# Setup of a decoder block: rotated biases ahead of two weights' low parts, and the value bias' output projection ahead of the int8 weights' transposes

## What is computed

```python
x = x + attn(layernorm(x), Wq, bq, Wk, bk, Wv, bv, Wo, bo)      # 16 heads, causal, RoPE on q and k
x = x + xattn(layernorm(x), ctx, wq, bq, wkv, bkv, wp, bp)      # q and output in fake int8 (qdq)
x = x + moe(layernorm(x), router_w, w_gate, w_up, w_down)       # 64 experts, top 8, capacity 128
# in attn:  q = rope(h @ Wq.T + bq);  k = rope(h @ Wk.T + bk);  v = h @ Wv.T + bv
#           y = softmax(q k / sqrt(d), causal) v;   return y @ Wo.T + bo
# in xattn: qdq(w) = clip(round(w / s), -127, 127) * s,  s = max(|row|) / 127
```

## Time and profile before

| | |
|---|---|
| median of 3 runs | 1580.34 us (1577.61 to 1582.30) |
| profiled execution | 1569.49 us, span from its first to its last instruction 1567.4 us |
| mean granted TensorE clock | 0.960 |
| PE busy | 1405.6 us (90%) |
| DVE busy | 1166.1 us (74%) |
| ACT busy | 970.7 us (62%) |
| POOL busy | 673.5 us (43%) |
| chain that ended last | PE 66%, DMA 23%, issue 5%, DVE 3% |

### The profile page before, as it was taken

The page is one execution under the profiler, slowest core; times in us unless marked ns, Lnnn a source line. Parts: engine busy times, 40 slices in busy tenths (PEclk is TensorE's granted clock), DMA queues, the critical chain, the costliest instruction groups (busy, mean ns, idle before and its releaser), DMA issues.

```text
span 1567.4 us, 35601 instructions
## 1 busy us (share of the span) xinstructions
PE 1405.6 (90%) x10963; PEld 1062.5 (68%) x10996; DVE 1166.1 (74%) x3111; ACT 970.7 (62%) x3345; POOL 673.5 (43%) x654
## 2 busy tenths in 40 slices
PE   3499999999999999999999999999719888888895
PEld 2367777777777777777777777777516555655573
DVE  5768888999899998999989999988624444444453
ACT  3357777777777777777777777777604333333342
POOL 0011454444544434535345453444443554555556
PEclk9799999999999999999999999999859999999998
DMA  9681233222211110111111011100597999999964
GB/s 294 255 312 42 97 136 119 99 105 88 90 40 38 41 34 27 27 34 35 39 27 27 27 34 41 33 21 22 187 328 220 284 266 279 283 273 281 265 100 50
DMA packets 159737, 195.80 MB, mean 125 GB/s; under 512 B 39541, under 2 KB 121845, under 8 KB 159680
## 3 DMA queue, kind: packets, MB, share of 16 engines
q1 hardware_dynamic: 120768, 157.27, 30.6%
q0 software_dynamic: 38912, 37.87, 11.9%
HBM read 127.60 MB, written 130.29 MB: 165 GB/s over the span
## 4 chain that ended last, share of the span: by engine, by line
PE 66%; DMA 23%; issue 5%; DVE 3%; ACT 1%; POOL 1%; SPq 1%; POOLq 0%; DVEq 0%
PE bank L502 34%; DMA out<-x,slots 20%; PE bank L527 7%; PE bank L484 7%; PE bank L520 5%; PE bank L534 4%; PE bank L508 3%; PE bank L540 2%; PE bank L515 2%; DMA x_in<-in_x 1%; PE bank L489 1%; DMA wide_b<-in_xkT_w 1%; POOL routed L1753 1%; ACT probs L966 1%; DMA probsT<-in_oT_w 1%
## 5 line engine op out<-in xcount | busy, mean ns | idle before, releaser
L966 ACT ACTIVATE probs<-bank,small 128x128 f32<-128x128 f32 x1024 | 362.1, 377 | 48.3 <-DVE small L1270 45.0
L1753 POOL DMA_INDIRECT routed<-row,slots x248 | 253.8, 1023 | 133.5 <-issue 73.7
L1822 POOL DMA_INDIRECT out<-x,slots x128 | 198.9, 1554 | 194.8 <-DMA out<-x,slots 140.5
L1718 POOL TENSOR_TENSOR small<-small,half 128x1 f32<-128x1 f32 x96 | 54.6, 569 | 523.6 <-DVE small L1242 523.6
L966 ACT ACTIVATION_READ_ACCUMULATOR probs<-bank,small 128x1 f32 x1024 | 220.7, 216 | 0.0
L960 ACT ACTIVATE probsT<-bank 128x512 f32<-128x512 f32 x256 | 143.9, 610 | 88.5 <-PE bank L527 88.5
L1270 DVE TENSOR_REDUCE small<-bank 128x4 f32<-128x512 f32 x256 | 166.7, 682 | 33.8 <-PE bank L520 33.8
L527 PE MATMUL bank<-idf,probs 128*128 128x128 f32 x1024 | 146.8, 277 | 2.7 <-ACT probs L966 2.4
L1673 DVE TENSOR_SCALAR slots<-pairs 128x1 uint32<-128x1 f32 x128 | 13.7, 149 | 172.0 <-DMA out<-x,slots 168.4
L527 PEld LDWEIGHTS bank<-idf,probs 128*128 128x128 f32 x1024 | 121.7, 144 | 27.0 <-DVE probs L1279 3.8
L1200 ACT ACTIVATE xn<-bank 128x192 f32<-128x192 f32 x64 | 21.3, 332 | 147.4 <-PE bank L906 147.4
(11 more groups left out here) (242 smaller groups left out, 3838.4 us busy)
## 6 DMA issues: line engine op xcount, KB each, us to landing
w_gate_up<-in_w_gate SPq DMA_DIRECT2D x128, 192.0 KB, 3.6
w_gate_up<-in_w_up SPq DMA_DIRECT2D x128, 192.0 KB, 3.9
w_down<-in_w_down SPq DMA_DIRECT2D x128, 192.0 KB, 4.3
routed<-empty_row SPq DMA_DIRECT2D x4, 5120.0 KB, 22.0
x_in<-in_x SPq DMA_DIRECT2D x32, 256.0 KB, 2.6
ctx_sb<-in_ctxT_in SPq DMA_DIRECT2D x32, 256.0 KB, 3.0
x_res<-in_x SPq DMA_DIRECT2D x32, 256.0 KB, 2.5
out<-x SPq DMA_DIRECT2D x32, 256.0 KB, 2.0
```

Of the source, the lines that this page charges most:

```text
L966: last = act.activation(probs[:, g, j * P:(j + 1) * P], bank[:, b, j * P:(j + 1) * P], ACT.Exp, bias=negated[:, h:h + 1], **({"accum_out": ...
L1753: pool.indirect_dma_start(routed, bass.IndirectOffsetOnAxis(ap=slots_of(m)[:, k:k + 1], axis=0), row_of(m)[:, :], None, bounds_check=SLOTS ...
L1822: pool.indirect_dma_start(out.rearrange("b p (h c) -> (b p h) c", h=2), bass.IndirectOffsetOnAxis(ap=place_of[k % 2][:, half_:half_ + 1], ...
```

## The change

On SP the two bias broadcasts move from behind weight 1 to behind the loads of `body(2)`, ahead of weights 4 to 7. On DVE the low parts of weights 4 and 5 move from ahead of the rotation of the biases to behind it. On PE the twelve matmuls of the value bias move to the head of `turn_quantised_weights`, into bank 7 instead of bank 0, behind a wait for the low parts and the spread value bias. DVE makes `att_bias` ahead of the scales' diagonal instead of behind everything, and PE's matmuls of line 868, which write the same bank 7, wait for it. ACT's counts shift by one; PE's wait for ACT's three copies now stands ahead of `body(3)`.

```diff
@@ sync
             stage_weights(0)
             stage_weights(1)
-            load_biases()
             stage_weights(2)
             stage_weights(3)
             load_constants()
             body(2)
+            load_biases()
             for n in range(len(STAGE), len(matrices_in)):
                 stage_weights(n)
@@ tensor
             def turn_quantised_weights():
+                pe.wait_ge(s_lo_dve, len(weights_in))
+                pe.wait_ge(s_vspread, 1)
+                project(7, attT_hi, attT_lo, "o", 0, True, False)
+                project(7, attT_hi, attT_lo, "o", 1, False, False)
+                project(7, attT_hi, attT_lo, "o", 2, False, True).then_inc(s_wT, 1)
                 for n, staged in enumerate((roped[:, :], packed[:, :])):
...
                 pe.wait_ge(s_wprep, 3)
+                pe.wait_ge(s_att, 1)
                 for g in range(KT):
...
                 last.then_inc(s_wT, 1)
-                pe.wait_ge(s_lo_dve, len(weights_in))
-                pe.wait_ge(s_wTr, 3)
-                pe.wait_ge(s_vspread, 1)
-                project(0, attT_hi, attT_lo, "o", 0, True, False)
-                project(0, attT_hi, attT_lo, "o", 1, False, False)
-                project(0, attT_hi, attT_lo, "o", 2, False, True).then_inc(s_wT, 1)
...
             pe.wait_ge(s_const, 16 * N_CONST)
-            pe.wait_ge(s_att, 1)
+            pe.wait_ge(s_wTr, 3)
             for cur in range(3, 7):
@@ scalar
-                act.wait_ge(s_wT, n + 1)
+                act.wait_ge(s_wT, n + 2)
...
-            act.wait_ge(s_wT, 3)
+            act.wait_ge(s_wT, 4)
             act.activation(xp_row[:, :], bank[:, 7, :], ACT.Copy).then_inc(s_wTr, 1)
...
-            act.wait_ge(s_wT, 4)
             for cur in range(3, 7):
@@ vector
             body(2)
-            weights_lo(4)
-            weights_lo(5)
             dve.wait_ge(s_ident, 16)
             dve.wait_ge(s_const, 16 * N_CONST)
             dve.wait_ge(s_bias, 32)
...
+            weights_lo(4)
+            weights_lo(5)
             spread_v = v_bias[:, :].unsqueeze(2).to_broadcast([P, KT, P])
...
+            dve.wait_ge(s_wT, 1)
+            dve.tensor_tensor(att_bias[:, :], bank[:, 7, :], xatt[:, :], ALU.add).then_inc(s_att, 1)
             for g in range(KT):
                 last = dve.tensor_scalar(xn2[:, g * P:(g + 1) * P], idf[:, :], xp_ws[:, g:g + 1], None, ALU.mult)
...
             dve.wait_ge(s_wT, 4)
-            dve.tensor_tensor(att_bias[:, :], bank[:, 0, :], xatt[:, :], ALU.add).then_inc(s_att, 1)
             for cur in range(3, 7):
```

## The result

The changed kernel took 1569.80 us (median of 11 runs, 1564.86 to 1574.18) where the kernel before, run beside it, took 1577.61 (11 runs, 1576.11 to 1582.30). The ratio is 0.9943, with an interval of 0.9931 to 0.9956: 9 us by the ratio, 7.8 by the medians. Most of those 2.3 us are the base: the forecast started from a median of three runs, 1580.34, and over 11 runs the kernel before has 1577.61. From that base the same difference gives 1569.4.

A forecast was written before the change was run, and what follows sets the result against it. Setup and pipeline filling ahead of DVE's `body(3)` were taken to bound the gain: 3.7 us from DVE's order plus 4.5 from PE's made 8.2, so 1580.34 became 1572.1 us; own range 1569.7 to 1574.5, full range 1567.5 to 1577.8.

The forecast's parts named there:

- What bounds, and where: Setup ahead of 62 us: idle holes on DVE and PE; the question was how much earlier DVE's `body(3)` starts.
- Part 1: SP's order: second x tile at 25.2 us, bias broadcasts priced at 1.6 us, o weight 0.57 us later.
- Rival 1: Broadcasts behind the x tile cost 3.7 to 5.2 us, giving 1574.2 to 1575.7 us; chance 0.18.
- Part 2: DVE's order: the 4.24 us bias rotation fills the hole, first row maximum 3.7 us earlier, at 38.5.
- The dear form: Broadcasts at 5.2 us, o weight landing at 36.9: DVE's reordering then gains only 0.1 us.
- Part 3: Value bias' twelve matmuls on PE move earlier, hidden behind DVE: 4.5 us off ahead of `body(3)`.
- The carry: Behind DVE's `body(3)`, the whole 8.2 us lead passes down the pipeline; clearing queue empty with 3.9 us margin.
- Its distance from the median: The runs' median stays 10.85 us above the profiled execution: 1561.3 profiled, 1572.1 median.
- rival 2: TensorE's clock still full at xp's transposes: 1.3 us more gain, 1570.8 us; chance 0.06.
- Rival 3: Fourth x tile lands at 96.3 whatever DVE does, queue still clearing: 1580.3 us, no change; chance 0.11.
- Rival 4: xq weight completes only with the clearing quarter issued behind it: 8.5 us slower, 1588.8; chance 0.05.
- Rival 5: Broadcasts land after DVE's hole, so DVE's reordering does nothing; no chance of its own.

The follow-up runs named there:

- the second pair of profiles: Kernel before and changed kernel profiled again on the third chip, nothing else changed: one run of 1578.62 us against a median of 1567.67, ratio 0.9944.
- PE's part alone: Kernel before with only the value bias' matmuls and `att_bias` moved, SP and DVE as before; ratios 0.9972 and 0.9973 to the kernel before.
- all but SP's: Changed kernel with one line, `load_biases()`, moved back to its early place; ratios 0.9960 and 0.9944 to the kernel before.

## Why the prediction was right

- **What bounds, and where.** Right: the lead is made ahead of 62 us. The hole on PE closed as described. DVE's two waits went from 3.42 us to 2.57, in three pieces; the gain came from taking the rotation off the path behind o, which is what the term counted.
- **Part 1.** The direction of each step was right, two sizes were not. The second x tile came at 24.44, not 25.2: its lead is 1.8 us, where only SP's issue time of 1.06 was counted. The tile's load is issued behind DVE's first x normalisation, which stands behind the low part of xk and had moved by 1.63 us (22.87 to 21.24); the working named that move and did not use it. The pair's price in the new place was set at 1.6 us, by its row among megabyte weights; in the same terms, from tile to o, it was 2.83, so o is 2.83 - 1.80 = 1.03 late, and over five executions the price was 2.3 to 4.4. The failing step is "in the new place, as in the old, megabyte weights stand in the queue beside the pair": ahead of the pair stand the twelve constants and the tile, and the windows of 101 to 166 GB/s were the nearer row. Rival 1, with 0.18, came near in two of five executions (prices of 4.1 and 4.4 in its range of 3.7 to 5.2); its own sign, o at 35 or later, was met in one (35.56, the other 34.89). The Trainium skill (DMA: Bandwidth & Descriptors, Queues, rings and completion order) was taken to make the cheap price the likelier; no trace here shows it in the new place, and none shows on which rings the time went.
- **Part 2.** 3.7 said, 3.21 measured (o 1.03 late instead of 0.57), 1.5 in the second pair of profiles (42.32 to 40.78). Of the signs, "no idle before xv's low part" failed (1.39 us) and "under 1 us before o's" held (0.35). The dear form was priced at 0.1 from o at 36.9; it came to 35.6 at most, since the tile came earlier than counted and the pair cost 4.4, not 5.2.
- **Part 3.** 4.5 said, 4.53 measured between the two profiled executions: 7.74 less 3.21. Over all executions the term was too small (4.5 to 6.7), because the old place ran at the half clock three times in four. The row of 3.15 us was one execution's, and nothing in the working bounded it from above. Wrong too was "over 2 us to spare, even at the half clock": 2.0 to 2.5 us is what PE waits for DVE's rounding where the matmuls run at full clock (2.46 in after), and 0.9 to 1.2 where they run at half clock (0.93 in the second profile). It was enough. This and part 2's shortfall are of opposite sign, which is part of why the sum came out.
- **The carry.** "Whole" was wrong by 2.2 us in the profiled pair. The clearing's queue took 33.29 us instead of 31.85, and set the fourth tile; that is 1.44. The 0.9 us that PE had lost by then (its mask took 1.89 us, in before 1.15) was hidden in DVE's wait for the tile. Another 0.8 went right behind the tile, where the twenty matmuls shown above took 6.48 us instead of 5.71: PE starts at half clock in after (granted 0.50 from 94 to 98 us) and at full clock in before, where it fell only within 101 to 102. In the second pair nothing was lost: from second normalise to 6th load it is 87.13 us before and 87.00 after. This stretch varies from 85.0 to 88.6 us over all kernels with two quarters in `body(3)`, so the loss is of the size of that scatter; it may still be more than that, since the five executions with both DVE's and PE's part have 88.0 in the mean and the four with the matmuls in their old place 86.5. With two executions each the lead at the 6th load is 6.6 us (143.46 against 150.06).
- **Its distance from the median.** The 10.85 us between before's profiled execution and its median were carried over, and this was no constant: after's profiled execution is 1.1 above its median. The forecast of a profiled 1561.3 missed by 9.6 us (1570.94), of which 3.4 is the one long instruction, 2.2 the carry and 0.5 part 2. The rest, some 3.5, went between the steady loop and the end of the experts, and no run says on what: the first output addition is at 1191.48 against 1190.95, the last 371.8 us behind it against 370.8. Only the forecast of the median, which needs the difference alone, held; and of the 10.85 us, 2.7 were its base of three runs.
- **Rivals 2 to 5.** The clock was not full at xp's transposes (row of scales 2.02 us), so rival 2 did not come. Rival 3 fell: the fourth tile moved by 6.3. Rival 4 fell: xq was there at 38.98. Rival 5 fell: with the pair in its new place the row maximum is 3.2 and 1.5 us earlier than in the profile of before beside it, not 0.1. That part 2 is worth something without SP's move is seen from PE's part alone against all but SP's, which differ by 1.5 and 1.8 us at the 6th load.
- **The sum by parts.** At the 6th load: PE's part 5.4 us, DVE's with it 1.6 more (144.6 to 143.0), SP's nothing, together 6.6 to 7.0. DVE's part is the one least sure: 2.9 us at the second normalise (57.8 to 54.9 in the means) have shrunk to these 1.6. The medians' 7.8 and the ratio's 9 are larger; the expert stage alone, from its first to its last output addition, varies between 370.8 and 378.3 us over all executions, which is too much for single traces to settle the difference. That the sum of 8.2 fell between the two is in part luck: part 2 and the carry were over-priced, part 3 under-priced.

Left open: why the loop's iterations took 40.9 us on two chips. On the third PE is busy for 32.95 of 33.00 us at a granted clock of 1.00; in the kernel without SP's part, on a slower one, for 36.31 of 40.90 at 0.92, so PE no longer sets the pace there. DVE stands 4.69 us ahead of the row maximum of the scores for a release that the profile calls remote; in after it is 0.85 us, for PE.

```profile
521.74 0.69 DVE L1269 TENSOR_REDUCE small<-bank 128x4 f32<-128x512 f32 x1 [4.69 <-remote]
```

```profile
520.83 0.69 DVE L1269 TENSOR_REDUCE small<-bank 128x4 f32<-128x512 f32 x1 [0.85 <-PE bank L520]
```

The setup's landmarks agree between the chips, so the readings of the setup above stand; the ratios of the kernel without SP's part from those two chips are 7 and 10 us over a longer time.

## What to carry to other kernels

Work that depends on nothing late but stands last on a chain is the cheapest gain: moving PE's twelve matmuls ahead of a wait that another engine sets anyway took them off the path at either clock, and made 5.4 of the 6.6 to 7 us at the 6th load. A row of before is one execution: where it carries a term, check whether the granted clock in its window could have been the other one, and price both levels. A transfer moved past short ones is priced by the windows with short transfers, not by those among large ones; and if moving it only makes another tile earlier that nobody waits for, leave it.

## What the hardware showed that I had not expected

- The same matmuls in the same place at 1.2 GHz in three executions (4.7 to 5.3 us) and at 2.4 in one (3.15).
- With eleven unread matmuls the stretch to the 6th load was 1.0 us shorter where they began at half clock and ended 0.34 us ahead of the real work, and no shorter where they began at full clock and ended 2.65 us ahead of it (one execution each).
- Two broadcasts of 256 KB landed 4.0 to 4.1 us after their issue in three executions and 5.7 in two, with the same order of loads; the same kernel shows both.
- One DVE instruction, 160 ns in the median, took 3.56 us once in 96, with no wait shown.
- Loop iterations of 40.9 us instead of 32.93 on two of three chips, with the setup unchanged.
